# Attention of a decoder layer: row sums taken two chunks later in one pass, other pairs joined, values in quarters of a block

## The reference

```
qkv = einsum('bnd,ed->bne', x, w_qkv);  q, k, v = to_heads(split(qkv, 3))     # 16 heads of 32
dots = einsum('bhnd,bhmd->bhnm', q, k) * SCALE
attn = softmax(dots, axis=-1)
out  = einsum('bhnm,bhmd->bhnd', attn, v)
out  = einsum('bnd,ed->bne', out, w_out) + b_out
x = layernorm(x + out)      # then cross-attention and the feed-forward part
```

## Time and profile before

| what | us |
|---|---|
| median of three timed executions | 1817.28 (1816.29 to 1817.51) |
| the profiled execution | 1825.24 |
| its span | 1823.4 |
| TensorE busy | 1770.6 (97%) |
| ScalarE busy | 1445.7 (79%) |
| VectorE busy | 1450.9 (80%) |
| first exponential of the attention to that of its last block | 294.12 to 1345.68 |

### The profile page before, as it was taken

One profiled execution on the slowest core, in us unless ns is written; L12 is line 12 of the kernel. 1 busy time (PEld: TensorE's weight loads), 2 busy tenths in 40 slices (PEclk: granted clock), 3 DMA queues, 4 the chain that ended last, 5 costly groups with the idle time before them and its releaser, 6 DMA issues. The chain is left out here.

```text
span 1823.4 us, 40231 instructions
## 1 busy us (share of the span) xinstructions
PE 1770.6 (97%) x15938; PEld 900.4 (49%) x15938; DVE 1450.9 (80%) x1582; ACT 1445.7 (79%) x1581; POOL 194.8 (11%) x189
## 2 busy tenths in 40 slices
PE   8999999999999999999999999999989999999997
PEld 6887885333333333333333333333346776644443
DVE  5345345988998898899998999989984778788898
ACT  5344356999999999999999999999964555555487
POOL 0000000010010010010010010010112221000044
PEclk9999999999999999999999999999999999999999
DMA  8665556658567577477566667676556340122075
GB/s 295 212 236 205 199 204 198 139 123 191 128 142 180 120 160 174 114 164 177 128 150 169 146 148 177 136 179 149 117 143 212 139 138 24 64 127 127 1 293 209
DMA packets 110832, 288.79 MB, mean 158 GB/s; under 512 B 8676, under 2 KB 25188, under 8 KB 97252
## 3 DMA queue, kind: packets, MB, share of 16 engines
q1 hardware_dynamic: 97012, 187.08, 28.7%
q0 software_dynamic: 13680, 99.62, 28.4%
HBM read 105.01 MB, written 82.05 MB: 103 GB/s over the span
## 5 line engine op out<-in xcount | busy, mean ns | idle before, releaser
L918 DVE TENSOR_TENSOR dve_sum<-dve_sum,probs 128x2048 f32<-128x2048 f32 x320 | 733.6, 2292 | 34.3 <-ACT probs L842 25.6
L842 ACT ACTIVATE probs<-score_others,shift_now 128x1536 f32<-128x1536 f32 x384 | 597.4, 1556 | 0.0
L1035 PE MATMUL mixed_ps<-probs,value_piece 128*32 128x512 f32 (+1 forms) x3840 | 402.9, 516 | 1.1 <-ACT probs L842 0.2
L841 ACT ACTIVATE probs<-score_first,shift_now 128x512 f32<-128x512 f32 x384 | 267.0, 695 | 2.2 <-PE score_others L997 1.1
L997 PE MATMUL score_first<-first_queries,key_piece 32*128 32x512 f32 x768 | 248.3, 429 | 4.3 <-ACT probs_paired L841 1.9
L997 PE MATMUL score_others<-first_queries,key_piece 32*128 32x512 f32 x2304 | 251.0, 429 | 0.0
L997 PE MATMUL score_others<-q_second,key_piece 32*128 32x512 f32 x2304 | 247.4, 424 | 0.0
L997 PE MATMUL score_first<-q_second,key_piece 32*128 32x512 f32 x768 | 245.1, 424 | 0.1
L997 PEld LDWEIGHTS score_first<-first_queries,key_piece 32*128 32x128 f32 x768 | 123.2, 185 | 186.0 <-ACT probs L841 94.9
L997 PEld LDWEIGHTS score_first<-q_second,key_piece 32*128 32x128 f32 x768 | 121.8, 183 | 183.4 <-ACT probs L841 105.4
L842 ACT ACTIVATE probs_paired<-score_others,shift_now 128x1536 f32<-128x1536 f32 x128 | 202.4, 1581 | 0.0
(11 more groups left out here) (253 smaller groups left out, 2581.7 us busy)
## 6 DMA issues: line engine op xcount, KB each, us to landing
probs_paired<-probs_paired POOLq DMA_DIRECT2D x95, 1024.0 KB, 8.4
o_scratch<-out_parts SPq DMA_DIRECT2D x33, 512.0 KB, 2.8
k_scratch<-parts SPq DMA_DIRECT2D x32, 512.0 KB, 4.6
q_scratch<-parts SPq DMA_DIRECT2D x32, 512.0 KB, 2.7
key_piece<-k_scratch SPq DMA_DIRECT2D x32, 512.0 KB, 5.1
h_scratch<-h SPq DMA_DIRECT2D x5, 2816.0 KB, 8.1
h<-h_scratch SPq DMA_DIRECT2D x5, 2816.0 KB, 11.5
v_scratch<-values SPq DMA_DIRECT2D x32, 256.0 KB, 2.0
```

Source lines behind the costliest of these rows:

```text
L841: nc.scalar.activation(block_probs(k)[:, 0:CH], score_first[:], ACT.Exp, bias=shift[:, c:c + 1], scale=SCALE).then_inc(probs_done, 1)
L842: nc.scalar.activation(block_probs(k)[:, CH:HPG * CH], score_others[n % 2][:], ACT.Exp, bias=shift[:, c:c + 1], scale=SCALE).then_inc(prob ...
L918: nc.vector.tensor_tensor(total[:], first[:], block_probs(k)[:], ALU.add).then_inc(dve_added, 1)
L1035: last = nc.tensor.matmul(mixed_ps[j * HD:(j + 1) * HD, lo:hi], v_group[k // KPP][:, k % KPP, j * HD:(j + 1) * HD], block_probs(k)[:, j * ...
```

## The change

- `PAIRS` becomes 9-10 and 13-14. Each pair is still joined by an accumulating DMA. The joined pairs are no longer added to each other: each is accumulated by a DMA onto `dve_sum`, the first after VectorE's last add of the chunk, the second after the first has landed. So there are four accumulating DMAs a chunk. A pair's two buffers are free when its sum has landed (`pair_free`).
- Row sums need one pass over `dve_sum`, in step 0 of the chunk after the next. A chunk's product waits one chunk longer for it, in one of two buffers `mixed`. In chunk 1 a pass over ones stands in its place.
- `VALUE_HALVES` becomes `VALUE_PARTS`, in quarters of 128 queries: 0, 4, 5, 4, 4, 5 and so on. Values begin in step 1.
- VectorE's copy of the product comes after the last add of the chunk.
- The value pieces are loaded as soon as they are read, in turn with the key pieces.
- The end has its own passes: the last chunk but one is summed into a piece of `score_others`, the last in five passes (a joined pair, three single blocks, VectorE's sum of eleven blocks). There is one store more.

```diff
-    PAIRS = ((2, 3), (4, 5))
+    PAIRS = ((9, 10), (13, 14))
-    SUM_PARTS = 2
-    SUMS_AT = ((0,), (1,))
+    BEHIND = 2
-    VALUE_HALVES = (0, 0, 2, 2, 3, 2, 2, 3, 2, 2, 3, 2, 2, 3, 2, 2)
+    VALUE_PARTS = (0, 4, 5, 4, 4, 5, 4, 4, 5, 4, 4, 5, 4, 4, 4, 4)
-        mixed = sb("mixed", [P, CH], F32)
+        mixed = [sb(f"mixed{u}", [P, CH], F32) for u in range(BEHIND)]
...
# SyncE
-                            sp.wait_ge(four_landed, 1 + (it + 1) * CPB)
-                            values_read(0)
-                            load_v(ng, nb, 0)
...
+                            for piece in range(PIECES):
+                                values_read(piece)
+                                load_v(ng, nb, piece)
+                                if piece + 2 < PIECES:
+                                    keys_read(piece + 2)
+                                    load_k(ng, nb, piece + 2)
...
# ScalarE
-                            if i is not None and k == PAIRS[i][1]:
-                                act.wait_ge(pairs_landed, it * CPB + c + 1)
-                            elif i == 0:
-                                act.wait_ge(four_landed, it * CPB + c + 1)
-                            elif i == 1:
-                                act.wait_ge(sums_done, it * CPB + c + 2)
+                            if i is not None:
+                                act.wait_ge(pair_free, 2 * (it * CPB + c) + 1 + i)
...
# VectorE, a chunk
+                def chunk(it, c, adds):
+                    take_shift(it if c == 0 else it + 1, (c + CPB - 1) % CPB)
+                    invert(it * CPB + c)
+                    divide(it * CPB + c, c)
+                    for a in range(adds):
+                        add(it, c, a)
+                with v.Fori(0, ITERS - 1) as it:
+                    for c in range(CPB):
+                        chunk(it, c, ADDS)
+                        gather(it, c + 1)
...
+                chunk(ITERS - 1, CPB - 1, ADDS - 1)
+                invert(CHUNKS, last_but_one_ps)
+                gather(ITERS - 1, CPB)
+                divide(CHUNKS, 0)
+                invert(CHUNKS + 1)
...
# GpSimd
+                def join_pair(it, c, i):
+                    into, other = PAIRS[i]
+                    pool.wait_ge(mixed_done, (it + 1) * BLOCKS + c * KB + into + 1)
+                    pool.wait_ge(probs_done, (it + 1) * EXPS + (c * KB + other + 1) * 2)
+                    pool.sem_inc(may_join, 1)
+                    nc.gpsimd.dma_start(probs_paired[i][0][:], probs_paired[i][1][:], accum_op=ALU.add).then_inc(pair_joined[i], 16)
+                def join_sum(it, c, i):
+                    f = it * CPB + c
+                    pool.wait_ge(pair_joined[i], 16 * (f + 1))
+                    if i == 0:
+                        pool.wait_ge(dve_added, (f + 2) * ADDS)
+                    pool.sem_inc(may_join, 1)
+                    nc.gpsimd.dma_start(dve_sum[c % 2][:], probs_paired[i][0][:], accum_op=ALU.add).then_inc(sum_joined, 16)
+                    if c == W_AT and i == 0:
+                        split_weights(it)
+                    pool.wait_ge(sum_joined, 32 * f + 16 * (i + 1))
+                    pool.sem_inc(pair_free, 1)
...
# TensorE
+                def sums(f):
+                    pe.wait_ge(mixed_copied, f + BEHIND)
+                    if f == 0:
+                        pe.sem_inc(sums_done, 1)
+                    elif f < BEHIND:
+                        fill().then_inc(sums_done, 1)
+                    else:
+                        pe.wait_ge(sum_joined, 32 * (f - 1))
+                        ones_times(mixed_ps, dve_sum[f % 2], True, True).then_inc(sums_done, 1)
+                def sums_last():
+                    pe.wait_ge(mixed_copied, CHUNKS + BEHIND)
+                    pe.wait_ge(probs_done, EXPS + CHUNKS * KB * 2)
+                    raw = [*PAIRS[1], ADD_ORDER[-1]]
+                    pe.wait_ge(pair_joined[0], 16 * CHUNKS)
+                    ones_times(mixed_ps, probs_paired[0][0], True, False)
+                    for k in raw:
+                        ones_times(mixed_ps, block_probs(k), False, False)
+                    pe.wait_ge(dve_added, (CHUNKS + 1) * ADDS - 1)
+                    ones_times(mixed_ps, dve_sum[(CHUNKS - 1) % 2], False, True).then_inc(sums_done, 1)
```

174 lines of the change are left out of this document (72 added, 102 removed).

## The result

The changed kernel takes 1799.26 us (median of four executions, 1796.33 to 1800.29) against 1817.39 us (1816.29 to 1818.31) of the kernel before: ratio 0.9886, 95% interval 0.987 to 0.9901. The quotient of the two medians alone is 0.990. The prediction was 1803. The profiled execution took 1800.29 us, 24.95 less than that of before (1825.24), where the sum of the prediction had 22.4 less.

What follows compares the result with a forecast made beforehand. ScalarE was taken to bound the attention stage at 2.007 us a block. 1028.3 against 1051.6 us gained 23.3, minus 0.9 at the end: 22.4 off the profiled 1825.24, so 1802.8, taken as 1803; range 1792 to 1816.

Steps and rivals of the forecast that it cites:

- The bound: Attention stage: ScalarE, by the ends of its exponentials, takes 2.007 us a block, 32.1 a chunk.
- at the pace of its starts: Rival on ScalarE's exponentials: starts 1.993 us apart are the true pace, 7 us less, 1796; 14%.
- Values in quarters: TensorE's value steps: the longest falls from 2.33 to 2.11 us, a quarter costing 0.22, so no ScalarE wait is left.
- Two chunks later: Row-sum pass no longer waits for a recent DMA: 11.9 us of stalls go, except 1.8 at the stage's start.
- VectorE's ring: VectorE's cycle from sum pass to sum pass takes 31.8 us, below ScalarE's 32.1, so hidden by 0.3 a chunk.
- The start: Start of the attention stage: 1.8 us lost at the low clock stays, and values beginning sooner add 0.9.
- Pairs and deadlines: Accumulating DMAs release pair buffers at 13.3 and 21.5 us, needed at 18.1 and 26.1: slack 4.8 and 4.6, ordinarily free.
- The slow chain in every chunk: Rival: the fourth DMA slows both accumulates everywhere; ScalarE stops 0.9 us in each of 31 chunks, +28, 1831; 9%.
- Loads in the plain order: Value pieces go out across an iteration's last chunk, needed 10 us or more later: free, but beside the accumulates.
- The rival of a collision at the turns: At iteration turns both accumulates take 12.0 us, released at 27.0 against 26.1; costs 6 to 12 us, about 1812; 13%.
- The end: End of attention, last exponential to last transpose of sums: 8.76 us becomes 9.7, costing 0.9.
- Profile and median: Timed median before is 8 us below its profile; if timed runs lack the first half's lumps, they come near 1802.8.

Runs made afterwards that it cites:

- The last two variants: Changed kernel with eighteen small TensorE products before the last sums, 1800.45 us; and with twelve, plus five-quarter value steps at 4, 7, 10 and 13, 1800.38 us.

## Why the prediction was right

**The bound.** ScalarE by the ends of its exponentials, 2.007 us a block, was the term that carried the sum: 2.009 measured. The rival "at the pace of its starts" is refuted as far as the runs go: over 511 blocks the starts are 2.009 apart too. They run 1.99 to 2.01 apart while the durations grow to 0.90 and 1.76, and then a jump behind a long step of TensorE takes back what they had gained; the ends keep 1.99 to 2.03 across it. The longest stretch without a jump was 14 blocks (in the run with two more reductions); whether the starts could go on at 1.99 beyond that was not measured.

**Values in quarters.** 2.11 forecast for the longest step, 2.11 measured; a quarter costs what the columns say, 0.21. The spacing of 2.17 by which I priced a long step (0.16) was read from starts, and four times 0.16 is 0.64, more than the 0.45 that I set out to explain; by the ends, 2.08 to 2.18 apart at these steps, it is about 0.11 each. The account of why the lumps cost was too narrow. I put the 0.45 us of an ordinary chunk on the steps of 2.33; the run with quarters alone shows that evening them out brings nothing while TensorE has 72 units a chunk. The arithmetic survived since it took the pass out as well (31.1 for TensorE's sum). By the runs, of the 0.43 some 0.25 are the changes other than the quarters, above all the one pass two chunks later, and 0.18 the quarters on top of them.

**Two chunks later.** The waits for DMAs went, as forecast, and 9.7 us of stalls with them. No run has the later pass without the new place of the pairs, so which of the two ended them is not shown. VectorE's ring was forecast at 31.8 and is 31.7; its copy waits 0.3 a chunk for TensorE, as forecast.

**The start failed, by 2.7 us.** The forecast kept 1.8 us of loss at the low clock and added 0.9. In the profiled execution nothing was lost. That was luck and no gain of the change: in the runs of the kernel before and its variants the first chunk took 32.06 to 34.84, in the changed one and its variants 31.98 to 36.5, and the kernel with the late loads, the same program up to there, had 35.23 against 31.98. It goes with the granted clock from 298 to 307 us: 1.00 goes with 31.98 to 32.35, 0.81 to 0.83 with 33.3 to 34.0, 0.62 to 0.66 with 34.6 to 35.2, 0.50 with 36.5. What sets this clock in one execution is open.

**Pairs and deadlines.** Issues at 3.0 forecast, 3.3 measured; the first addition 10.3, or 12.0 at a turn, forecast, 10.4 and 12.6 measured; no wait, as forecast. The slack of 4.8 that I gave the first pair is 4.4 by the rows (released at 13.7, wanted at 18.1) and 2.2 at a turn. Moving the pairs agrees: two positions, 4.0 us, earlier (7-8) the ordinary chunks still don't wait and nearly all turns do; three, 6.0 us, earlier half of all chunks do, and the undisturbed ones escape since there the first addition takes only 7.6. The slow chain in every chunk did not come; the DMA share of 0.86 (forecast 0.84) did no harm at these deadlines.

**Loads in the plain order.** "Free in itself" held. What the prediction did not see is that the old order would have cost 32 us with the new joins, and the plain order 34 us with the old ones. The rival of a collision at the turns had the right mechanism for the wrong combination: with the old joins the loads hold up the joins, with the new joins and the old order it is the DMAs of the joins that hold up the loads, and in the chunks shown each wait is followed by the low clock.

**The end failed, without a price.** 0.9 more was forecast, 3.0 came: VectorE's tenth addition waited 0.46 for ScalarE, and after 2.12 us of idleness TensorE did the last passes in part at the lower clock, 1.3 + 0.5 us too long. The clock is of this execution: with the late loads it stayed up, and the transposition came 10.03 after the last exponential, 1.3 more than before. The terms of the forecast add up to 39.45, not 39.8 (32.4 + 1.7 + 0.7 + 5 x 0.93), so by themselves they gave 0.6. The next stage gave it all back, its first `mix_z` coming 32.4 us after that transposition and not 36.1; why, no run shows.

**Profile and median.** The forecast took its time from the profile on the ground that timed executions lack the stalls. Neither profile of the kernel before lacks them, and timed executions without them were not seen. The timed gain is 18.1 us and the profiled one 24.95: the first profile of before, 1825.24, was longer than the executions beside it, but in the later runs single executions of the same kernel reached 1828.2, with medians of 1820.4 to 1821.6. The last two variants, which take within 1.2 us of the changed kernel's time, are 20.0 and 21.1 us below the medians beside them, so the first four executions of before were on the short side. That 1803 came near 1799.26 is in part luck. The gain of the profile was forecast 2.5 too small by errors that partly cancel: 2.7 at the start and 1.2 at the end too little, 0.8 in the bound and 0.6 ahead of the stage too much. And the time was taken from a profile 8 us above its median. What the runs bear out is the gain per block and the end of the stalls.

## What to carry to other kernels

When two engines are both full, even out the lumps of one only together with taking work from it: here neither paid in full alone. A transfer's deadline and the order of the loads that run beside it are one decision; try each with the other's old setting before calling either free. And the slack of a ring is measured by adding work until the period moves, not by the idle time in front of one instruction.

## What the runs showed of the hardware

ScalarE's durations in the trace are no cost. The spacing stayed at 2.009 us while the mean durations were 0.83 and 1.69, together 0.52 more; the page of the changed kernel has

```profile
L833 ACT ACTIVATE probs<-score_others,shift_now 128x1536 f32<-128x1536 f32 x384 | 650.6, 1694 | 0.0
...
L832 ACT ACTIVATE probs<-score_first,shift_now 128x512 f32<-128x512 f32 x384 | 320.2, 834 | 1.1 <-PE score_others L1003 1.1
```

That is an overlap of 0.26 us on average for each instruction. The Trainium skill (ScalarE: Activation LUTs, What ACT_TABLE_LOAD costs) gives about 93 ns for it; here the rows decide.

An accumulating DMA of 1 MB on GpSimd's queue held the next one up for 7.6 us when it ran alone, 10.4 beside another, and 12.6 beside another and loads of keys and values; a load of 256 KB of values took a median of 5.4 us in the kernel before, 7.3 in the changed one and 10.9 where it went out beside two such DMAs.

The same idle time of TensorE can cost its clock or not: at the end of the attention it was followed by a granted clock of 0.50 to 0.51 in three profiles (idle for 2.12, 2.21 and 2.37 us) and by 1.00 in nine (1.79 to 2.65 us), and the kernel before had one of each. A loss at the low clock that one profile shows is no fixed part of a kernel's time.
